# A GRU recurrence turned from hidden units on partitions to sequences on partitions

## The chip, the core and the metric

The kernel is one program on one core of a Trainium2 chip. Its engines run side by side, each through its own list of instructions, and meet at semaphores: PE (TensorE, matmuls), DVE (VectorE), ACT (ScalarE), POOL (GpSimd) and SP (SyncE, which here only issues DMAs). The metric is the time of one execution on the device in microseconds.

## What is computed

Input x has 16 sequences of 256 steps and 512 features. Layer 0 adds a feed-forward block to x: a conditioning vector for each sequence (attention over block sums, projected) is added, the rows are normalised, quantised in blocks of 32, and go through gate, up and down matrices (512 to 2048 and back), quantised again in between. Layer 1 runs a GRU over the 256 steps and adds a linear layer with 16 low-rank experts, of which a router picks two. The part that the change touches is the GRU:

```python
def cell(h, x):
    gi = x @ W_ih + b_ih
    gh = h @ W_hh + b_hh
    i_r, i_z, i_n = jnp.split(gi, 3, axis=-1)
    h_r, h_z, h_n = jnp.split(gh, 3, axis=-1)
    r = jax.nn.sigmoid(i_r + h_r)
    z = jax.nn.sigmoid(i_z + h_z)
    n = jnp.tanh(i_n + r * h_n)
    h_new = (1.0 - z) * n + z * h
    return (h_new, h_new)
```

Here h is 16 by 512 and W_hh is 512 by 1536. Each step needs the state of the step before, so 256 steps follow one another.

## The kernel before

The work is cut into 32 tiles of 128 rows, a row being one sequence at one step, so a tile holds 8 steps. Every engine walks through slots (c, s), where c is the tile in recurrence and s from 0 to 7 is its step. Beside step s of tile c a slot holds pieces of the other stages for neighbouring tiles: Q (normalising and quantising tile c+4), F (feed-forward of tile c+3), E (the end of the feed-forward and x1 of tile c+2), I (the input product x1 @ W_ih of tile c+1), R (the recurrence of tile c) and L (the expert layer of tile c-1). The order on each engine is the order in which `slot` and `others` write it. There is no scheduler, and no instruction passes another of its engine.

The recurrence before keeps hidden units on partitions. W_hh is the stationary operand in 128 by 128 pieces, and 32 columns stream past each: 16 columns of the high half of the state in half precision and 16 of its low half. Weights are split in two halves as well. A step takes 3 gates times 4 output pieces times 4 inner pieces times 2 halves, 96 matmuls (`state_products`, L1248, called at L1282 to L1284). The gates r and n lie in `ps_rn`, z lies in `ps_z`. DVE (`recur`, L709) adds the two halves and the input terms, ACT takes three tanh, and DVE forms the new state with 64 numbers on each of 128 partitions, rounds it (`hT`, L753) and takes the low half (L704), for which PE waits (L1280).

The input product `x_wih` (L1139) has W_ih stationary and 128 columns of x1 moving, 144 matmuls for a tile. ACT moves its result out with bias and scale (L512), so that `gi` lies with units on partitions, as the recurrence wants it. The scale of x1 is one number for the tile: a row maximum on DVE (L852), a turn of it by PE (`max_row`, L1108), a maximum over the row (L856), and a matmul that spreads the result (`spread_scale`, L1115). Four fp32 transposes turn x1 (L1125), and ACT and DVE split it in halves out of PSUM (L499, L901).

On DVE, `others(c, s, 0)` stands ahead of the step's first instruction, and places 1, 2 and 3 stand after the first additions, after `n_pre` and after the new state. Below, place 0 to 3 has this meaning.

## Time and profile before

| | |
|---|---|
| median of 3 runs | 1842.02 us (1841.2 to 1842.82) |
| profiled execution, own time | 1841.74 us |
| its span in the trace | 1839.9 us |
| PE busy | 1609.0 us, 87% of the span |
| PE weight loads busy | 1252.7 us, 68% |
| DVE busy | 1511.1 us, 82% |
| ACT busy | 661.5 us, 36% |
| POOL busy | 511.7 us, 28% |

Busy time is the union of an engine's instructions, and an engine that is busy need not be at its best rate. The first 326 us load, quantise and fill the pipeline of stages, then the 256 steps run to 1821 us. Rows of the trace below give times in microseconds from the start of the span, and L numbers are lines of the kernel before.

### The profile page before, as it was taken

Reading aid. Unit: us, or ns where it says so; the run is one execution under the profiler, and the core shown is the slowest. Engines: PE = TensorE matmul, PEld = TensorE weight load, DVE = VectorE, ACT = ScalarE, POOL = GpSimd, SP = SyncE. Lnnn points to the kernel's source line nnn. Section 1 sums busy time; section 2 is a strip of 40 time slices with the busy share of each in tenths; the row PEclk is TensorE's granted clock in tenths of the full one; section 3 lists DMA queues with packets and bytes.
Section 4 is the critical chain, followed back from the end, with each engine's and each line's share of the span. In section 5 each row is a group of like instructions: output and inputs, shape, how many; then the busy total and the mean of one; then the engine's idle time right before and its main releaser. Section 6 shows DMA issues by size and latency. Waiting matters only on the chain.

```text
span 1839.9 us, 76467 instructions
## 1 busy us (share of the span) xinstructions
PE 1609.0 (87%) x32972; PEld 1252.7 (68%) x32972; DVE 1511.1 (82%) x5651; ACT 661.5 (36%) x1712; POOL 511.7 (28%) x571
## 2 busy tenths in 40 slices
PE   5422246899999999999999999999999999999986
PEld 2211114788777777877777777787777877778874
DVE  8999988888888888888888888888888888887654
ACT  1111123444443434344343444434434344334331
POOL 4445423222222222222222222222222222221001
PEclk8755568999999999999999999999999999999997
DMA  6413121000100010000000100000000000000000
GB/s 250 162 63 132 54 92 32 29 9 32 31 32 32 32 32 32 32 32 32 32 26 31 32 32 31 32 32 32 32 32 32 32 31 32 26 26 24 22 15 19
DMA packets 35411, 80.12 MB, mean 44 GB/s; under 512 B 4865, under 2 KB 5249, under 8 KB 34689
## 3 DMA queue, kind: packets, MB, share of 16 engines
q1 hardware_dynamic: 28080, 63.09, 9.8%
q10 hardware_dynamic: 6992, 12.13, 1.9%
q8 instruction: 260, 4.26, 1.0%
q14 instruction: 79, 0.64, 0.1%
HBM read 58.43 MB, written 16.78 MB: 41 GB/s over the span
## 4 chain that ended last, share of the span: by engine, by line
PE 72%; DVE 23%; issue 2%; ACT 1%; DMA 1%; POOL 0%; DVEq 0%; ACTq 0%; SPq 0%; POOLq 0%
PE ps_rn L1254 22%; PE ps_gi L1148 11%; PE ps_z L1254 9%; PE ps_gate_up L1087 6%; PE ps_down L1105 6%; PE ps_base L1157 4%; PE ps_gate_up L1081 4%; PE ps_base L1201 3%; PE ps_route L1157 3%; DVE gi L567 2%; DVE gi L564 1%; DVE wam L541 1%; DVE gi L569 1%; DVE wm L564 1%; DVE fe L766 1%
## 5 line engine op out<-in xcount | busy, mean ns | idle before, releaser
L1254 PE MATMUL ps_rn<-hT,whh 128*128 128x32 f16 x16320 | 449.0, 176 | 37.1 <-DVE hT L704 37.0
L1254 PEld LDWEIGHTS ps_rn<-hT,whh 128*128 128x128 f16 x16320 | 434.9, 96 | 63.6 <-DVE hT L704 56.2
L976 POOL TENSOR_TENSOR qf<-f8c,fe 128x512 bf16<-128x512 bf16 x128 | 135.6, 1059 | 902.5 <-DVE f8c L783 885.8
L1148 PE MATMUL ps_gi<-x1T,wih 128*128 128x128 f16 x4608 | 288.6, 219 | 1.2 <-ACT gi L512 1.2
L1148 PEld LDWEIGHTS ps_gi<-x1T,wih 128*128 128x128 f16 x4608 | 270.3, 98 | 25.7 <-issue 1.7
L521 ACT ACTIVATE r_tanh<-r_pre,scale_half 128x64 f32<-128x64 f32 x256 | 89.0, 348 | 452.1 <-DVE r_pre L724 452.1
L1254 PE MATMUL ps_z<-hT,whh 128*128 128x32 f16 x8160 | 243.3, 176 | 0.0
L1254 PEld LDWEIGHTS ps_z<-hT,whh 128*128 128x128 f16 x8160 | 222.7, 96 | 0.0
L512 ACT ACTIVATE gi<-ps_gi,b_i,scale_x 128x128 f32<-128x128 f32 x384 | 144.4, 456 | 200.7 <-PE ps_gi L1148 200.7
L718 DVE TENSOR_TENSOR r_half<-ps_rn,gi 128x64 f32<-128x64 f32 x256 | 56.6, 221 | 143.8 <-PE ps_rn L1254 143.7
L1081 PE MATMUL ps_gate_up<-wq,qxT 128*128 128x512 bf16 x512 | 136.0, 389 | 13.3 <-DVE inter L798 13.3
L523 ACT ACTIVATE z_tanh<-z_pre,scale_half 128x64 f32<-128x64 f32 x256 | 89.0, 348 | 161.3 <-DVE z_pre L734 161.3
L1087 PE MATMUL ps_gate_up<-wq,qxT 128*128 128x512 bf16 x512 | 138.2, 394 | 2.1 <-ACT sg_gs L472 2.1
L1105 PE MATMUL ps_down<-wq,qfT 128*128 128x512 bf16 x512 | 133.3, 383 | 0.0
L1157 PE MATMUL ps_base<-wl,hT 128*128 128x512 f16 x384 | 97.1, 391 | 0.0
L525 ACT ACTIVATE n<-n_pre,scale_half 128x64 f32<-128x64 f32 x256 | 89.0, 348 | 12.3 <-DVE n_pre L741 1.0
L798 DVE TENSOR_TENSOR inter<-ps_gate_up,sg_gs 128x512 f32<-128x512 f32 x128 | 87.3, 682 | 7.2 <-PE ps_gate_up L1087 7.0
L759 DVE TENSOR_REDUCE fam<-inter 128x16 f32<-128x512 f32 x128 | 87.8, 686 | 4.4
L472 ACT ACTIVATE sg_gs<-ps_gate_up 128x512 f32<-128x512 f32 x128 | 74.1, 579 | 42.8 <-PE ps_gate_up L1081 42.8
L777 DVE SCALAR_TENSOR_TENSOR f<-inter,finv 128x512 fp8e4<-128x512 f32 x128 | 87.6, 684 | 0.0
L1087 PEld LDWEIGHTS ps_gate_up<-wq,qxT 128*128 128x128 bf16 x512 | 43.1, 99 | 59.9 <-issue 27.5
L1105 PEld LDWEIGHTS ps_down<-wq,qfT 128*128 128x128 bf16 x512 | 48.4, 99 | 49.5 <-issue 4.1
(200 smaller groups left out, 2680.2 us busy)
## 6 DMA issues: line engine op xcount, KB each, us to landing
wih<-in_x_steps ACTq DMA_DIRECT2D x32, 256.0 KB, 5.3
xin<-in_x_steps SPq DMA_DIRECT2D x32, 256.0 KB, 3.5
...
```

The costliest lines, as they stand in the source:

```text
L512: last = nc.scalar.activation(gi_gate(i, g)[:, k, :], ps_gi[:, k * P:(k + 1) * P], ACT.Identity, bias=b_i[:, g * KD + k:g * KD + k + 1], s ...
L521: nc.scalar.activation(r_tanh[:, :], r_pre[:, :], ACT.Tanh, scale=HALF_S_INV).then_inc(r_ok, 1)
L523: nc.scalar.activation(z_tanh[:, :], z_pre[:, :], ACT.Tanh, scale=HALF_S_INV).then_inc(z_ok, 1)
L525: nc.scalar.activation(n[:, :], n_pre[:, :], ACT.Tanh, scale=HALF_S_INV).then_inc(n_ok, 1)
L759: v.tensor_reduce(am[:, :], blocked(src[:, :]), AX_X, ALU.max, apply_absolute_value=True).then_inc(small, 1)
L976: g.tensor_tensor(blocked(qf[:, :]), blocked(f8c[:, :]), spread(fe16[:, :]), ALU.mult).then_inc(qf_done, 1)
L1081: last = mm(ps_gate[:, :], qxT[:, k, :], w_ffn(0, n, k), start=k == 0, stop=k == KD - 1)
L1087: last = mm(ps_up[:, :], qxT[:, k, :], w_ffn(8, n, k), start=k == 0, stop=k == KD - 1)
L1105: last = mm(ps_down[:, :], qfT[:, i, :], w_down(i), start=i == 0, stop=i == NF * KD - 1)
L1148: last = mm(ps_gi[:, j * P:(j + 1) * P], wih_parts[:, k, at:at + P], x1T[:, x, k, :], start=k + w + x == 0, stop=k == KD - 1 and w == 1)
L1157: last = mm(out, hT[l % 2][:, 2 * k + x, :], wl_parts[:, k, begin:begin + n], start=k + w + x == 0, stop=stop and w == 1)
L1254: last = mm(ps[:, (at + j) * 2 * B:(at + j + 1) * 2 * B], whh[:, k, u, gate * D + j * P:gate * D + (j + 1) * P], hx(t)[:, 2 * k:2 * k + 2, ...
```

## The change

Sequences go on partitions in the recurrence. The 512 hidden units are four groups of 128, and group g of all 16 sequences lies on partitions 32g to 32g+15. The state is now stationary (16 columns) and W_hh streams: 384 columns (three gates of one group) for each matmul. The four groups write to four column tiles of the PE array, partitions 0, 32, 64 and 96 of one PSUM bank. A step is 48 matmuls: high state by high weights and high state by low weights (32 of them), a wait for the low state, and low state by high weights (16). Two banks `ps_gru` alternate. DVE works on 128 columns for each gate: one addition of 256 columns for r and z, one of 128 for n, and at the end a 32 by 32 block transpose of the new state, from which both halves are taken.

The input product now has x1 stationary and W_ih moving with 512 columns, 36 matmuls a tile. DVE moves its result out (place 0 of steps 2, 4, 6), rows on partitions. Since a step needs its 16 rows on the partitions of the four groups, SP sends four DMAs of 24 KB for each step, from `gi` to a ring of four steps, two slots ahead. The scale of x1 is one number for each row, so that PE's two small matmuls and their way back go. x1 is split in halves before it is turned, by ACT and DVE, and eight half-precision transposes turn it. Biases are spread by matmuls once, ahead of the recurrence, and weights are loaded in another order of rows. The load of x1 for the expert layer and its result share one tile, and its load moves from slot 0 to slot 2 on SP.

```diff
+GROUPS, GROUP = 4, 32
+RING = 4
...
-        ps_rn, ps_z, ps_up, ps_down = bank("ps_rn"), bank("ps_z"), bank("ps_gate_up"), bank("ps_down")
+        ps_gru = bank("ps_gru0"), bank("ps_gru1")
+        ps_up, ps_down = bank("ps_gate_up"), bank("ps_down")
...
+        gi_ring = sb("gi_ring", [P, RING, 4 * P])
+        h, hT_both = sb("h", [P, P]), sb("hT_both", [P, KD, GROUP])
...
+            def load_gi(t):
+                c, s = t // STEPS, t % STEPS
+                sp.wait_ge(gi_ev, count(c, 3, 3))
+                wait(sp, n_pre_ok, t - RING + 1)
+                if t < RING:
+                    sp.wait_ge(ring_clear, 1)
+                for g in range(GROUPS):
+                    sp.dma_start(gi_ring[g * GROUP:g * GROUP + B, t % RING, 0:3 * P],
+                                 gi_tokens(c)[s * B:(s + 1) * B, g, :, :].rearrange("p q f -> p (q f)"))\
+                        .then_inc(gi_in[t % RING], 16)
...
+                if 0 <= c * STEPS + s + 2 < T:
+                    load_gi(c * STEPS + s + 2)
...
+                if (c, s) == (-2, 7):
+                    act.wait_ge(wih_lo, KD)
+                    for gate in range(3):
+                        act.wait_ge(bias_mm, gate + 1)
+                        nc.scalar.activation(gi_bias[:, gate * D:(gate + 1) * D], (ps_gi, *ps_gru)[gate][:, :], ACT.Copy,
+                                             scale=S_WH).then_inc(bias_ok, 1)
...
+                if E and s == 6:
+                    act.wait_ge(x_small, count(e, 6, 5))
+                    wait(act, x_mm, count(e, 1))
+                    nc.scalar.activation(x1_parts[:, 0, :], x1[:, :], ACT.Copy, scale=S_X[:, :]).then_inc(x_hi, 1)
                 if E and s == 7:
-                    act.wait_ge(x_scale_mm, count(e, 1, 1))
-                    wait(act, x_ev, count(e, 1))
-                    wait(act, gi_ev, count(e, 3))
-                    nc.scalar.activation(scale_x[:, :], ps_x_scale, ACT.Copy).then_inc(x_scale_ok, 1)
                     act.wait_ge(x_mm, count(e, 1, 1))
                     wait(act, gi_mm, count(e, 3))
-                    act.wait_ge(x_scale_ok, count(e, 1, 1))
-                    nc.scalar.activation(x1T[:, 0, :, :], ps_turn[:, :].rearrange("p (k n) -> p k n", k=KD),
-                                         ACT.Copy, scale=S_X).then_inc(x_hi, 1)
+                    nc.scalar.activation(x1T[:, :, :, :], turn_x.rearrange("p (u k n) -> p u k n", u=2, k=KD),
+                                         ACT.Copy).then_inc(x_ev, 1)
...
-                    for k in range(KD):
-                        last = nc.scalar.activation(gi_gate(i, g)[:, k, :], ps_gi[:, k * P:(k + 1) * P], ACT.Identity,
-                                                    bias=b_i[:, g * KD + k:g * KD + k + 1], scale=X_TO_WH)
-                    last.then_inc(gi_ev, 1)
...
+                    t = c * STEPS + s
+                    act.wait_ge(rz_pre_ok, t + 1)
+                    nc.scalar.activation(r_tanh[:, :], pre[:, 0:P], ACT.Tanh, scale=HALF_S_INV).then_inc(r_ok, 1)
+                    nc.scalar.activation(z_tanh[:, :], pre[:, P:2 * P], ACT.Tanh, scale=HALF_S_INV).then_inc(z_ok, 1)
+                    act.wait_ge(n_pre_ok, t + 1)
...
+            def state_parts(t):
                 dve.wait_ge(h_ok, t + 2)
-                v.tensor_tensor(h_part(t, 1), by_chunk(h[:, :]), h_part(t, 0), ALU.subtract).then_inc(hx_ok, 1)
-            def gi_step(c, gate, s):
-                return gi_gate(c, gate)[:, :, s * B:(s + 1) * B]
+                v.transpose(hT_both[:, :, :].rearrange("p k b -> p (k b)"), h[:, :]).then_inc(h_turned, 1)
+                dve.wait_ge(h_turned, t + 2)
+                v.tensor_copy(h_part(t, 0), hT_both[:, :, 0:B]).then_inc(hx_hi, 1)
+                dve.wait_ge(hx_hi, t + 2)
+                v.tensor_tensor(h_part(t, 1), hT_both[:, :, 0:B], h_part(t, 0), ALU.subtract).then_inc(hx_ok, 1)
...
+                t = c * STEPS + s
+                dve.wait_ge(gh_mm, t + 1)
+                dve.wait_ge(gi_in[t % RING], (t // RING + 1) * GROUPS * 16)
+                if t < RING:
+                    dve.wait_ge(bias_ok, 3 + RING)
+                v.tensor_tensor(pre[:, 0:2 * P], ps_gru[t % 2][:, 0:2 * P], gi_step(t)[:, P:3 * P],
+                                ALU.add).then_inc(rz_pre_ok, 1)
+                v.tensor_tensor(pre[:, 2 * P:3 * P], ps_gru[t % 2][:, 2 * P:3 * P], gi_step(t)[:, 3 * P:4 * P],
                                 ALU.add).then_inc(hn_ok, 1)
                 beside(1)
+                dve.wait_ge(hn_ok, t + 1)
+                dve.wait_ge(r_ok, t + 1)
+                v.scalar_tensor_tensor(rn[:, :], r_tanh[:, :], 1.0, pre[:, 2 * P:3 * P], ALU.add,
+                                       ALU.mult).then_inc(rn_ok, 1)
+                dve.wait_ge(rn_ok, t + 1)
+                v.scalar_tensor_tensor(n_pre[:, :], gi_step(t)[:, 0:P], 2.0, rn[:, :], ALU.mult,
                                        ALU.add).then_inc(n_pre_ok, 1)
                 beside(2)
                 if s == 0:
                     wait(dve, base_mm, c - 1)
+                dve.wait_ge(z_ok, t + 1)
                 v.tensor_scalar(less_z[:, :], z_tanh[:, :], 1.0, HALF_S_H, ALU.subtract, ALU.mult)
                 v.scalar_tensor_tensor(zh[:, :], z_tanh[:, :], 1.0, h[:, :], ALU.add, ALU.mult).then_inc(zh_ok, 1)
+                dve.wait_ge(zh_ok, t + 1)
+                dve.wait_ge(n_ok, t + 1)
                 v.tensor_tensor(zn[:, :], less_z[:, :], n[:, :], ALU.mult).then_inc(zn_ok, 1)
+                dve.wait_ge(zn_ok, t + 1)
                 v.scalar_tensor_tensor(h[:, :], zh[:, :], 0.5, zn[:, :], ALU.mult, ALU.subtract).then_inc(h_ok, 1)
+                state_parts(t)
...
+                if E and here == (6, 3):
+                    dve.wait_ge(x_hi, count(e, 1, 1))
+                    v.scalar_tensor_tensor(x1_parts[:, 1, :], x1[:, :], S_X[:, :], x1_parts[:, 0, :], ALU.mult,
+                                           ALU.subtract).then_inc(x_lo, 1)
+                if I and place == 0 and s in (2, 4, 6):
+                    g = s // 2 - 1
+                    dve.wait_ge(gi_mm, count(i, 3, g + 1))
+                    if c == -1:
+                        dve.wait_ge(bias_ok, 3)
+                    v.scalar_tensor_tensor(gi_tokens(i)[:, :, gi_place(g), :], ps_gi[:, :].rearrange("p (g f) -> p g f", g=GROUPS),
+                                           x_to_wh[i % 2][:, :], gi_bias[:, g * D:(g + 1) * D].rearrange("p (g f) -> p g f", g=GROUPS),
+                                           ALU.mult, ALU.add).then_inc(gi_ev, 1)
...
-                mm(ps_x_row, row_max[:, :], idf[:, :], start=True, stop=True).then_inc(x_row_mm, 1)
...
-                mm(ps_x_scale, ones_row[:, :], x_row[:, :], start=True, stop=True).then_inc(x_scale_mm, 1)
...
+                for u in range(2):
+                    for k in range(KD):
+                        at = (u * KD + k) * P
+                        last = turn_(turn_x[:, at:at + P], x1_parts[:, u, k * P:(k + 1) * P], idh[:, :])
...
+                for k in ks:
+                    for w, x in PART_PRODUCTS:
+                        at = w * GATES + n * D
+                        last = mm(ps_gi[:, :], x1T[:, x, k, :], wih_parts[:, k, at:at + D], start=k + w + x == 0,
+                                  stop=k == KD - 1 and w == 1)
...
+            def state_products(t):
+                def by_group(w, u):
                     for k in range(KD):
+                        gates = whh[:, k, w, :].rearrange("p (q g f) -> p q g f", q=3, g=GROUPS)
+                        for g in range(GROUPS):
+                            last = mm(ps_gru[t % 2][g * GROUP:g * GROUP + B, 0:3 * P], hx(t - 1)[:, 2 * k + u, :],
+                                      gates[:, :, g, :], start=k + w + u == 0, stop=u == 1 and k == KD - 1)
+                    return last
+                by_group(0, 0)
+                by_group(1, 0)
+                pe.wait_ge(hx_ok, t + 1)
+                by_group(0, 1).then_inc(gh_mm, 1)
...
+                    t = c * STEPS + s
+                    wait(pe, hn_ok, t - 1)
+                    pe.wait_ge(hx_hi, t + 1)
+                    state_products(t)
...
```

PE, ahead of a middle tile's step 5 and up to step 6. First before: `ps_rn` and `ps_z` are the 96 state products, `ps_gi` the input product.

```order
L1254 MATMUL ps_rn<-hT,whh 128x32 x64
L1254 MATMUL ps_z<-hT,whh 128x32 x32
L1113 MATMUL ps_route<-idf,row_max 1x128
L1087 MATMUL ps_gate_up<-wq,qxT 128x512 x4
L1105 MATMUL ps_down<-wq,qfT 128x512 x4
L1148 MATMUL ps_gi<-x1T,wih 128x128 x24
L1254 MATMUL ps_rn<-hT,whh 128x32 x64
```

The same place of PE after the change, where `ps_gru` holds the 48 state products.

```order
L1258 MATMUL ps_gru<-whh,hT 16x384 x48
L1111 MATMUL ps_gate_up<-wq,qxT 128x512 x4
L1129 MATMUL ps_down<-wq,qfT 128x512 x4
L1158 MATMUL ps_gi<-wih,x1T 128x512 x6
L1258 MATMUL ps_gru<-whh,hT 16x384 x48
```

The turn of the row maximum is gone, 96 narrow matmuls became 48 wide ones, and 24 of the input product became 6.

DVE before, step 6 of a middle tile: from the place 0 pieces to the low half of the state.

```order
L798 TENSOR_TENSOR inter<-ps_gate_up,sg_gs 128x512
L759 TENSOR_REDUCE fam<-inter 128x16
L838 TENSOR_TENSOR wxa<-xa,coeff 128x256
L856 TENSOR_REDUCE x_max<-ps_route 1x1
L718 TENSOR_TENSOR r_half<-ps_rn,gi 128x64
L720 TENSOR_TENSOR hn_half<-ps_rn,b_h 128x64
L724 TENSOR_TENSOR r_pre<-ps_rn,r_half 128x64
L727 TENSOR_TENSOR hn<-ps_rn,hn_half 128x64
```

DVE after, the same place; `pre_activations` is the sum of state product and ring.

```order
L817 TENSOR_TENSOR inter<-ps_gate_up,sg_gs 128x512
L778 TENSOR_REDUCE fam<-inter 128x16
L857 TENSOR_TENSOR wxa<-xa,coeff 128x256
L882 TENSOR_SCALAR x_scale<-x_inverse 128x1
L883 TENSOR_SCALAR x_to_wh<-x_power,scale_l 128x1
L894 SCALAR_TENSOR_TENSOR gi<-ps_gi,x_to_wh,wih 128x4x128
L750 TENSOR_TENSOR pre_activations<-ps_gru,gi_ring 128x256
L752 TENSOR_TENSOR pre_activations<-ps_gru,gi_ring 128x128
```

A third of the input product's way out now stands ahead of the step's first addition, and two additions took the place of four.

The end of the same step on DVE after the change:

```order
L772 TENSOR_TENSOR zn<-less_z,n 128x128
L774 SCALAR_TENSOR_TENSOR h<-zh,zn 128x128
L736 STREAM_TRANSPOSE hT_both<-h 128x128
L738 CAST hT<-hT_both 128x4x16
L740 TENSOR_TENSOR hT<-hT_both,hT 128x4x16
L887 SCALAR_TENSOR_TENSOR x_parts<-x,x_scale,x_parts 128x512
```

Between the new state and the half that PE waits for, a transpose and a rounding now stand, and the low half of x1 follows at place 3.

## Rows read from the trace of the kernel before

**Rows 1.** Page part 5: line, engine, shapes, count; busy us, mean ns; idle before, releaser.

```profile
L1254 PE MATMUL ps_rn<-hT,whh 128*128 128x32 f16 x16320 | 449.0, 176 | 37.1 <-DVE hT L704 37.0
L1254 PEld LDWEIGHTS ps_rn<-hT,whh 128*128 128x128 f16 x16320 | 434.9, 96 | 63.6 <-DVE hT L704 56.2
```

**Rows 2.** Windows: stretch, its length, then PE, PEld, DVE, ACT, POOL busy; clock; DMA.

```profile
300.00:350.00 50.00, 45.24 (x827) 34.91 (x825) 43.32 (x136) 22.44 (x53) 15.76 (x16) 0.97 0.07 24
...
1750.00:1800.00 50.00, 39.21 (x1097) 33.96 (x1094) 29.27 (x154) 16.21 (x48) 2.69 (x6) 0.93 0.05 13
...
1000.00:1200.00 200.00, 196.93 (x4311) 158.14 (x4308) 164.29 (x703) 81.24 (x221) 54.52 (x67) 1.00 0.09 29
```

**Rows 3.** Source L704, low half of the state: durations, first and last start.

```profile
L704 DVE TENSOR_TENSOR hT<-h,hT x256: 224/225/227, 326.2 to 1820.7; 128x64 f16<-128x64 f32 x128
```

**Rows 4.** Timeline of PE, one tile: start, length, group, count, [idle before].

```profile
1005.32 1.77 PE L1254 MATMUL ps_rn<-hT,whh 128*128 128x32 f16 x64 [0.59 <-DVE hT L704]
...
1007.73 1.02 PE L1087 MATMUL ps_gate_up<-wq,qxT 128*128 128x512 bf16 x4
...
1014.71 1.50 PE L1148 MATMUL ps_gi<-x1T,wih 128*128 128x128 f16 x24
1016.05 0.81 PE L1157 MATMUL ps_base<-wl,hT 128*128 128x512 f16 x3
...
1019.18 0.38 PE L1113 MATMUL ps_route<-idf,row_max 128*1 128x128 f32 x2
1019.49 1.04 PE L1087 MATMUL ps_gate_up<-wq,qxT 128*128 128x512 bf16 x4
1020.36 1.03 PE L1105 MATMUL ps_down<-wq,qfT 128*128 128x512 bf16 x4
...
1052.86 1.77 PE L1254 MATMUL ps_rn<-hT,whh 128*128 128x32 f16 x64 [0.59 <-DVE hT L704]
```

**Rows 5.** Waits from 1001.4 to 1048.95: who waited for whom, total, times, longest.

```profile
DVE r_half L718 <- PE ps_rn L1254: 3.8, 5, 1.3
...
DVE x1T L901 <- ACT x1T L499: 1.3, 1, 1.3
```

**Rows 6.** Timeline of DVE, one step of the tile.

```profile
1007.12 0.22 DVE L718 TENSOR_TENSOR r_half<-ps_rn,gi 128x64 f32<-128x64 f32 x1 [0.73 <-PE ps_rn L1254]
1007.26 0.21 DVE L720 TENSOR_TENSOR hn_half<-ps_rn,b_h 128x64 f32<-128x64 f32 x1
...
1010.12 0.22 DVE L755 SCALAR_TENSOR_TENSOR h<-zh,zn 128x64 f32<-128x64 f32 x1
1010.38 0.22 DVE L704 TENSOR_TENSOR hT<-h,hT 128x64 f16<-128x64 f32 x1
```

**Rows 7.** Lines by form, 600 to 1600 us: shapes, count; busy, mean ns; idle.

```profile
L777 DVE SCALAR_TENSOR_TENSOR f<-inter,finv 128x512 fp8e4<-128x512 f32 x85 | 58.2, 684 | 0.0
...
L472 ACT ACTIVATE sg_gs<-ps_gate_up 128x512 f32<-128x512 f32 x84 | 48.5, 577 | 0.0
...
L897 DVE SCALAR_TENSOR_TENSOR y<-ps_base,scale_l,x_bias 128x512 f32<-128x512 f32 x21 | 15.8, 751 | 0.0
```

**Rows 8.** Timeline of all engines near the end, one step with nothing beside it.

```profile
1785.09 1.79 PE L1254 MATMUL ps_rn<-hT,whh 128*128 128x32 f16 x64 [0.73 <-DVE hT L704]
...
1786.91 0.23 DVE L718 TENSOR_TENSOR r_half<-ps_rn,gi 128x64 f32<-128x64 f32 x1 [1.69 <-PE ps_rn L1254]
...
1788.63 0.35 ACT L525 ACTIVATE n<-n_pre,scale_half 128x64 f32<-128x64 f32 x1
...
1790.02 1.79 PE L1254 MATMUL ps_rn<-hT,whh 128*128 128x32 f16 x64 [2.33 <-DVE hT L704]
```

**Rows 9.** Timelines of DVE and of GpSimd where both run.

```profile
1001.95 0.88 DVE L766 TENSOR_SCALAR fe<-fam 128x16 f32<-128x16 f32 x1
...
1001.53 1.27 POOL L988 TENSOR_TENSOR xg<-xg,beta_b 128x512 f32<-128x512 f32 x1
```

**Rows 10.** DMA issues: KB each, us from issue to landing.

```profile
h<-in_h SPq DMA_DIRECT2D x1, 32.0 KB, 1.6
```

274 lines of the change are left out of this document (105 added, 169 removed).

## The prediction

> **What bounds the kernel now.** I read the costliest groups first. The state products wait 37 us in all for the low half of the state [rows 1], of 256 steps. Then the windows: from 1000 to 1200 us PE is busy 196.9 of 200 and DVE 164.3 [rows 2]. The 256 steps lie between 326.2 and 1820.7 us [rows 3]. In the timeline of PE one tile of eight steps runs from 1005.32 to 1052.86, 47.54 us, with one idle gap of 0.59 [rows 4]. The reader is to see PE going from one group to the next. So PE sets the end in a middle tile, but DVE is close behind it: in this tile it waits 3.8 us for `ps_rn` and 1.3 for ACT's turned x1 [rows 5], and fills the other 42.4 us with work and short gaps. Near the end no other stage is left, and a step takes 4.93 us, from PE's start at 1785.09 to 1790.02 [rows 8]: that is the loop itself, products, additions, tanh, new state. 29 tiles at 47.54 and 23 steps at 4.93 make 1492 of the 1494.5 us between first and last state, which is how I use the two figures.
>
> So there are three limits for a tile: PE's work (47.0), DVE's work and the waits that it cannot fill, and the loop (8 times 4.93, 39.4). The change lowers the first and raises the other two.
>
> **PE's part.** The 96 products take 2.41 us (1005.32 to 1007.73) [rows 4]. The new ones stream 12 rounds of 384 columns, if the four column tiles run side by side. A 512-column matmul takes 0.217 (four in 0.87, from 1019.49 to 1020.36) [rows 4], so 384 take 0.163 and a round no less: 1.95 us a step. That saves 0.46, 3.7 a tile. The row-maximum matmul takes 0.31 (1019.18 to 1019.49) [rows 4]; with the other one like it, 0.6 a tile. The input product: 24 matmuls of 128 columns take 1.34 (1014.71 to 1016.05) [rows 4], 144 take 8.0, and 36 of 512 columns 7.8: 0.2. Four fp32 turns against eight in half precision I count even. PE's tile goes from 47.0 to 42.5 us.
>
> No row shows a column tile. The bounds for one step are 1.95 us (all four together) and 48 times 0.163, 7.8 us (none together). I take 1.95, because weight loads last 96 ns each [rows 1] where a load and its matmul follow every 0.025 us (64 in 1.6), so several are under way at once, and four independent tiles need one pair started only every 0.041.
>
> **DVE's part.** In the step at 1007.12 an instruction of 64 columns starts 0.14 after one that it does not need and 0.26 after one that it needs (1010.12 to 1010.38) [rows 6]. A 512-column one lasts 0.684 against 0.22 [rows 6, 7], 1.04 ns a column; 64 more columns are 0.07, 192 more 0.20. Before, a step has 14 instructions, 9 of the first kind and 5 of the second: 2.56 us. After there are 11: the sum for r and z 0.34; hn, `n_pre`, `less_z` 0.21 each; rn, zh, zn, h and the transpose 0.33 each, since each is needed at once; high half 0.26; low half 0.14. That is 3.02, so 0.46 more a step, 3.7 a tile. The input product's way out leaves ACT, which had room, and costs DVE three times 0.67 (0.751 long as `y` [rows 7], less the overlap of 0.08 that the rows show between a length of 0.22 and a distance of 0.14), 2.0 a tile. The low half of x1 replaces an equal one. The small scale steps lose some 0.2. Occupied: 42.4 + 3.7 + 2.0 - 0.2 = 47.9 us, already above the old tile.
>
> Waits that DVE cannot fill: from the sum's start to r's tanh in hand are 0.42 + 0.40 + about 0.10 in hand-overs, 0.92 (tanh of 64 columns lasts 0.35 [rows 8], 512 columns 0.577 [rows 7]; 0.40 is my estimate for 128). DVE has 0.55 of its own there; 0.37 stays in steps 1, 3 and 7, which have nothing at place 1: 1.1. In step 3 place 0 is short (1.2) and PE's results come 2.14 after its start: 0.7. In step 6 the low half of x1 waits for ACT, whose turn comes after tanh, silu and two copies: 0.4. Together 2.2. Two waits of before go: `ps_rn`, since DVE now arrives later than PE nearly everywhere, and x1T. The tile comes to 50.1 us, 2.55 longer, over 29 tiles 74 us.
>
> The three pieces of `gi` stand at place 0 of steps 2, 4 and 6, ahead of the sum that starts the loop. Behind them in DVE's queue waits the whole step, for which ACT and PE wait in turn. Step 6 has inter, its maxima, wxa and `gi` there, over 3 us against 2.14 for PE. So the saving on PE buys nothing in these steps: late next is DVE.
>
> **The unknown prices on DVE.** The transpose of 128 by 128 fp32: at least the 0.26 of a 64-column instruction, at most the 0.72 of a 512-column one; I take 0.33 because it reads and writes 128 columns. This leaves -18 to +100 us over 256 steps. The conversion of the high half may be held up: `fe` takes 0.88 instead of some 0.17 when it starts at 1001.95 inside a GpSimd instruction from 1001.53 to 1002.80 [rows 9]. GpSimd is busy 54.5 of 200 us [rows 2]; a hold of 0.35 on average in 27% of 256 steps is 25 us, against 0. I keep it in the range.
>
> **The loop, where nothing else runs.** Before 4.93. After: products 1.95 and 0.19 until DVE has them, as `r_half` starts 1.82 after PE's start with 1.63 of products ahead of it [rows 8]; r's tanh in hand 0.92; rn 0.33; `n_pre` to n in hand 0.79; zn, h, transpose 1.0; high half and PE's start 0.28. Sum 5.46, 0.53 more. The loop now needs all three gates before the first addition, where r and n alone used to do. 23 steps make 12 us.
>
> **What hides.** 1024 new DMAs of 24 KB: the load of `h`, 32 KB, landed 1.6 us after its issue [rows 10], and they go out two slots (12 us) ahead. At a tile's edge SP stands at the store of y until DVE's last instruction of step 7, and the next ring load behind it still has two slots. Cost 0; without the cover up to 2 us a tile, 64. ACT has less to do (its copies of `gi` go, x1T is one copy of 1024 columns); cost 0. Ahead of the first step come 16 matmuls to spread biases, seven ACT copies, a memset and 27 more load DMAs, in a stretch where PE is busy 45.2 of 50 and DVE 43.3 [rows 2]. I take 5 us, from 0 to 12.
>
> **Sum.** 74 + 12 + 5 = 91 on the profiled execution's own 1841.7 us (span 1839.9): 1933. The median of the runs, 1842.0, differs by 0.3 and changes nothing.
>
> **Two rules that speak against it.** The loads of 128 columns overlap matmuls on the same rows of the array [rows 1, 4]. The Trainium skill, TensorE: Matmul & The Clock Gate, Part 3, says that a weight load overlaps matmuls in flight only when its row group differs; the four column tiles share all rows, so by that rule the first rival below would come. By it the trace would not show what it shows, and its table nevertheless has three column tiles running 2.38 times faster, which no run here shows yet.
>
> PE's result is there 0.176 us after the start of a 32-column matmul, of which 0.025 is its turn [rows 1]; so emptying the array costs up to 0.15, and twice a step. The Trainium skill, TensorEngine Tiling (Array Packing), Key Properties, says that a change of tiling mode drains the engine. One of the two falls in time in which PE waits anyway. The other is off the loop and takes 1.2 a tile of the 7.6 that PE has over. It would add some 5 to 10 us to 1933.
>
> **Rival 1: the tiles do not run side by side.** Then a step is 7.8 + 0.19 + 3.32, with 0.3 of DVE's delays 11.6 us, times 256, and 351 around them: 3320. In favour: nothing in the trace shows them together. Against: the overlapping loads. If they overlap by two, products take 3.9, a step about 7.7, and the time is 2320; with 2.5 to 3 us it is 1990 to 2100, since DVE's place 0 covers the first half microsecond. The skill's rule on row groups, above, leads to 3320.
>
> **Rival 2, the other side: wide instructions cost DVE little more than narrow ones.** The mechanism is the fixed part, 0.14 of distance, if width counted only beyond it. If the chain's 128-column instructions cost what those of 64 do, a step loses 0.8, the tile falls under 44, PE's 42.5 and its drains become the bound, and 29 tiles save some 100 us: about 1750. It decides from 0.32 us a step on. Against it stands 0.684 for 512 columns. A smaller error of mine, or pieces that fill waits better, would end between 1790 and 1838.
>
> **Rival 3: the clock.** It is 1.00 with PE at 98%, 0.97 at 45.2 of 50 and 0.93 at 39.2 of 50 [rows 2], and 1.2 GHz is its lower level. PE will work 42.5 of 50 us. At 0.95 its products lengthen by 0.1 a step, 25 us: 1960.
>
> **How the numbers follow.** DVE-bound as worked out, 1885 to 1990, rival 3 in it: 0.62. The same with less loss, 1846 to 1885: 0.06. Partly overlapping tiles, 1990 to 2500: 0.13. None overlapping: 0.07. Faster (rival 2 and its smaller forms): 0.10. Within 0.2%, about what a measurement of this kernel can tell from no change: 0.02. So faster 0.10, same 0.02, slower 0.88. The range 1855 to 2110 leaves out the serial case, the faster one and the far end of the partial one.
>
> **What would show it.** The period of a middle tile near 50 (not 47.5, not 44); PE idle 5 to 7 us of it, before the state products, with DVE's conversion as releaser; 48 products in about 2.1 us; the sums on DVE waiting for PE only in steps 0 and 3; the transpose near 0.28 long; the last steps 5.4 to 5.5 apart. A period under 47 with DVE waiting would refute the DVE ledger; products over 3 us the overlap; a sum released by a DMA the cover.

## The result, and the profile after

The changed kernel takes 1974.91 us (median of 4 runs, 1971.5 to 1976.78) against 1841.61 us (1838.99 to 1842.82) for the kernel before: a ratio of 1.0724, 95% interval 1.071 to 1.0738. It is 133 us slower. Predicted were 1933 us, range 1855 to 2110, with a chance of 0.88 for slower. In the profiled execution the span is 1969.5 us.

First the page after, part 5 as in [rows 1], and one row of part 6:

```profile
L1258 PE MATMUL ps_gru<-whh,hT 128*16 128x384 f16 x12240 | 568.4, 337 | 230.7 <-DVE hT L738 229.5
L1258 PEld LDWEIGHTS ps_gru<-whh,hT 128*16 128x16 f16 x12240 | 311.0, 91 | 499.3 <-issue 357.5
...
L750 DVE TENSOR_TENSOR pre_activations<-ps_gru,gi_ring 128x256 f32<-128x256 f32 x256 | 107.2, 419 | 92.0 <-PE ps_gru L1258 89.7
...
L758 DVE SCALAR_TENSOR_TENSOR rn<-r_tanh,pre_activations 128x128 f32<-128x128 f32 x256 | 77.2, 301 | 39.7 <-ACT r_tanh L559 36.9
L761 DVE SCALAR_TENSOR_TENSOR n_pre<-gi_ring,rn 128x128 f32<-128x128 f32 x256 | 99.4, 388 | 8.8
...
L736 DVE STREAM_TRANSPOSE hT_both<-h 128x128 f32<-128x128 f32 x257 | 80.0, 311 | 8.8
...
gi_ring<-gi SPq DMA_DIRECT2D x1024, 24.0 KB, 1.9
```

PE's wait for the state has grown from 37 to 230 us: the bound has moved off PE. `n_pre` is 388 ns on average where its neighbours of the same width are 295 to 301; that is the first hint of what the prediction did not place. The chain that ended last (page part 4) gives the same picture; before, PE had 72% of it and DVE 23%:

```profile
DVE 61%; PE 21%; issue 9%; ACT 7%; DMA 1%; DVEq 0%; POOL 0%; ACTq 0%; SPq 0%; POOLq 0%
```

The low half of the state (L740 now; columns as in [rows 3]) shows where the time lies:

```profile
L740 DVE TENSOR_TENSOR hT<-hT_both,hT x256: 224/224/228, 326.5 to 1950.3; 128x64 f16<-128x64 f32 x128
```

The first state comes 0.3 us later than before, the end 19.2 us after the last as before, and the 256 steps take 129.3 us more. Eight starts of that line are one tile. The first tile takes 56.1 us (before 47.7), the next 27 tiles 51.17 on average (before 47.57; 50.6 in some, 51.9 to 52.2 in about every third), the last three together 140.9 (before 126.6), and the last seven steps 45.2 (before 35.9). So 8.5 + 97.3 + 14.3 + 9.3 us.

The windows (columns as in [rows 2]), first two short ones inside a tile that takes 52 us:

```profile
1006.00:1009.40 3.40, 1.21 (x6) 0.36 (x4) 3.12 (x10) 1.27 (x4) 1.46 (x2) 1.00 0.01 3
1009.40:1012.80 3.40, 2.83 (x36) 1.36 (x40) 1.65 (x5) 0.25 (x2) 1.05 (x1) 0.50 0.33 87
...
1000.00:1200.00 200.00, 174.63 (x2052) 87.57 (x2051) 176.15 (x570) 61.09 (x154) 50.27 (x61) 0.98 0.15 43
```

In 200 us PE is busy 174.6 instead of 196.9, DVE 176.2 instead of 164.3. The two short windows are step 2 and the start of step 3 of that tile. Here are DVE, then POOL (GpSimd), then PE in that place (start, length, instruction, idle before it):

```profile
1004.75 0.42 DVE L750 TENSOR_TENSOR pre_activations<-ps_gru,gi_ring 128x256 f32<-128x256 f32 x1
1005.08 0.28 DVE L752 TENSOR_TENSOR pre_activations<-ps_gru,gi_ring 128x128 f32<-128x128 f32 x1
1005.28 0.93 DVE L785 TENSOR_SCALAR fe<-fam 128x16 f32<-128x16 f32 x1
1006.24 0.17 DVE L787 TENSOR_SCALAR finv<-fe 128x16 uint32<-128x16 uint32 x1
1006.33 1.25 DVE L790 TENSOR_SCALAR fe<-fe 128x16 uint32<-128x16 uint32 x1
1007.49 0.28 DVE L758 SCALAR_TENSOR_TENSOR rn<-r_tanh,pre_activations 128x128 f32<-128x128 f32 x1
```
```profile
1004.91 1.27 POOL L1011 TENSOR_TENSOR xg<-xn,gamma_b 128x512 f32<-128x512 f32 x1 [4.91 <-DVE xn L907]
1006.26 1.29 POOL L1013 TENSOR_TENSOR xg<-xg,beta_b 128x512 f32<-128x512 f32 x1
```
```profile
1009.97 3.50 PE L1258 MATMUL ps_gru<-whh,hT 128*16 128x384 f16 x48 [2.77 <-DVE hT L738]
1013.40 0.82 PE L1111 MATMUL ps_gate_up<-wq,qxT 128*128 128x512 bf16 x3
```

Two operations on 16 columns take 0.93 and 1.25 us, where the same lines take 0.17 in other steps. Each starts inside a GpSimd pass over 512 columns and ends 0.03 us after that pass (1006.18 and 1007.55). The whole chain of the step stands behind them. PE runs out of work, idles for 2.77 us, and the granted clock is 0.50 (1.2 GHz) from 1009.4 to 1012.8, so the next 48 products take 3.50 us instead of 2.13. In step 7 the same happens to an operation of the chain itself:

```profile
1039.45 0.40 DVE L758 SCALAR_TENSOR_TENSOR rn<-r_tanh,pre_activations 128x128 f32<-128x128 f32 x1 [0.34 <-ACT r_tanh L559]
1039.89 1.24 DVE L761 SCALAR_TENSOR_TENSOR n_pre<-gi_ring,rn 128x128 f32<-128x128 f32 x1
```
```profile
1038.66 1.05 POOL L1001 TENSOR_TENSOR qf<-f8c,fe 128x512 bf16<-128x512 bf16 x1 [5.71 <-DVE f8c L802]
1039.66 1.31 POOL L994 TENSOR_TENSOR xs<-xin,proj 128x512 f32<-128x512 f32 x1
```

Added up, these holds are 0.76 + 1.08 + 0.12 + 0.95 = 2.9 us a tile (0.12 is `rn` above, which starts inside the first of the two passes). They come in every tile from the second to the 27th, 2.8 to 2.9 us in all but one. The clock does not fall in every tile: it falls behind step 2 in 9 of the 27 middle tiles.

What DVE waits for, 600 to 1700 us, some 21.5 tiles:

```profile
DVE pre_activations L750 <- PE ps_gru L1258: 31.9, 22, 2.5
...
DVE rn L758 <- ACT r_tanh L559: 21.8, 64, 0.3
DVE x_parts L887 <- ACT x_parts L543: 7.0, 21, 0.3
```

That is 0.34 for r's tanh in three steps of a tile, 0.33 for the high half of x1 in one, and one wait for the products a tile, in step 3 (the prediction had expected it in step 0 too). No wait for a DMA is among them. And a step of the tail, with nothing beside the loop:

```profile
1899.60 2.13 PE L1258 MATMUL ps_gru<-whh,hT 128*16 128x384 f16 x48 [1.59 <-DVE hT L738]
...
1901.78 0.42 DVE L750 TENSOR_TENSOR pre_activations<-ps_gru,gi_ring 128x256 f32<-128x256 f32 x1 [1.40 <-PE ps_gru L1258]
...
1902.74 0.29 DVE L758 SCALAR_TENSOR_TENSOR rn<-r_tanh,pre_activations 128x128 f32<-128x128 f32 x1 [0.34 <-ACT r_tanh L559]
...
1905.24 0.99 PE L1258 MATMUL ps_gru<-whh,hT 128*16 128x384 f16 x20 [1.77 <-DVE hT L738]
```

From product to product 5.64 us; before it was 4.93 [rows 8].

### The profile page after: what moved, and what is told of

The parts are those of the page before. It is cut to its first block, busy times and chain, and to the rows that moved or that the text cites. A ratio compares the mean times of both kernels' runs of the same rounds, so it can differ in the third digit from the quotient of the medians.

```text
span 1969.5 us, 45556 instructions
## 1 busy us (share of the span) xinstructions
PE 1543.6 (78%) x17268; PEld 773.2 (39%) x17268; DVE 1689.1 (86%) x4947; ACT 559.1 (28%) x1335; POOL 521.4 (26%) x573
## 4 chain that ended last, share of the span: by engine, by line
DVE 61%; PE 21%; issue 9%; ACT 7%; DMA 1%; DVEq 0%; POOL 0%; ACTq 0%; SPq 0%; POOLq 0%
PE ps_gru L1258 14%; DVE n_pre L761 5%; DVE pre_activations L750 4%; DVE rn L758 3%; DVE hT_both L736 3%; DVE inter L817 3%; DVE zn L772 3%; DVE h L774 3%; DVE gi L894 3%; ACT n L562 2%; ACT r_tanh L559 2%; PE ps_route L1167 2%; DVE hT L738 2%; DVE fe L790 2%; DVE f L796 2%
## 5 line engine op out<-in xcount | busy, mean ns | idle before, releaser
L1258 PE MATMUL ps_gru<-whh,hT 128*16 128x384 f16 x12240 | 568.4, 337 | 230.7 <-DVE hT L738 229.5
L1258 PEld LDWEIGHTS ps_gru<-whh,hT 128*16 128x16 f16 x12240 | 311.0, 91 | 499.3 <-issue 357.5
L559 ACT ACTIVATE r_tanh<-pre_activations,scale_half 128x128 f32<-128x128 f32 x256 | 102.8, 401 | 920.4 <-DVE pre_activations L750 920.4
L1158 PE MATMUL ps_gi<-wih,x1T 128*128 128x512 f16 x1152 | 280.3, 379 | 1.3 <-DVE gi L894 1.3
L750 DVE TENSOR_TENSOR pre_activations<-ps_gru,gi_ring 128x256 f32<-128x256 f32 x256 | 107.2, 419 | 92.0 <-PE ps_gru L1258 89.7
L562 ACT ACTIVATE n<-n_pre,scale_half 128x128 f32<-128x128 f32 x256 | 102.7, 401 | 207.2 <-DVE n_pre L761 207.2
L1158 PEld LDWEIGHTS ps_gi<-wih,x1T 128*128 128x128 f16 x1152 | 109.5, 98 | 118.2 <-issue 3.5
L761 DVE SCALAR_TENSOR_TENSOR n_pre<-gi_ring,rn 128x128 f32<-128x128 f32 x256 | 99.4, 388 | 8.8
L560 ACT ACTIVATE z_tanh<-pre_activations,scale_half 128x128 f32<-128x128 f32 x256 | 98.9, 386 | 0.0
L736 DVE STREAM_TRANSPOSE hT_both<-h 128x128 f32<-128x128 f32 x257 | 80.0, 311 | 8.8
```

Of the source, the lines that this page charges most:

```text
L559: nc.scalar.activation(r_tanh[:, :], pre[:, 0:P], ACT.Tanh, scale=HALF_S_INV).then_inc(r_ok, 1)
L562: nc.scalar.activation(n[:, :], n_pre[:, :], ACT.Tanh, scale=HALF_S_INV).then_inc(n_ok, 1)
L736: v.transpose(hT_both[:, :, :].rearrange("p k b -> p (k b)"), h[:, :]).then_inc(h_turned, 1)
L750: v.tensor_tensor(pre[:, 0:2 * P], ps_gru[t % 2][:, 0:2 * P], gi_step(t)[:, P:3 * P], ALU.add).then_inc(rz_pre_ok, 1)
L761: v.scalar_tensor_tensor(n_pre[:, :], gi_step(t)[:, 0:P], 2.0, rn[:, :], ALU.mult, ALU.add).then_inc(n_pre_ok, 1)
L1158: last = mm(ps_gi[:, :], x1T[:, x, k, :], wih_parts[:, k, at:at + D], start=k + w + x == 0, stop=k == KD - 1 and w == 1)
```

## The experiments

All kernels but e16 and e18 start from the changed kernel. e1, e2, e3, e4, e12 and e16 leave something out or compute something else; the others compute everything. "Tile" is the mean of the second to the 28th tile of the recurrence in the profiled execution, the ratio is to the kernel before, timed on the same chip. The changed kernel has 1974.9 us, 1.0724 and 51.17.

| run | us | ratio, 95% interval | tile |
|---|---|---|---|
| e1_one_column_tile | 3337.1 (one run) | | 93.64 |
| e2_no_transpose | 1910.2 | 1.0368 (1.0351 to 1.0386) | 49.41 |
| e3_gate_inputs_by_scalar | 1924.2 | 1.0439 (1.0422 to 1.0456) | 49.67 |
| e4_no_shared_hold | 1900.2 | 1.0310 (1.0292 to 1.0327) | 48.93 |
| e5_keep_clock | 1953.8 | 1.0625 (1.0607 to 1.0642) | 50.60 |
| e6_reordered | 1894.7 | 1.0298 (1.0281 to 1.0315) | 48.63 |
| e8_all_together | 1904.9 | 1.0356 (1.0338 to 1.0373) | 49.05 |
| e10_early_split | 1974.2 | 1.0727 (1.0709 to 1.0745) | 51.32 |
| e12_fewer_products | 1942.8 | 1.0545 (1.0523 to 1.0567) | 50.92 |
| e13_bias_on_tensor | 1868.7 | 1.0139 (1.0121 to 1.0158) | 47.85 |
| e16_before_no_hold | 1814.4 | 0.9843 (0.9825 to 0.9861) | 46.85 |
| e18_before_reordered | 1819.9 | 0.9880 (0.9863 to 0.9896) | 46.86 |

**e1: one column tile.**

```diff
-mm(ps_gru[t % 2][g * GROUP:g * GROUP + B, 0:3 * P], ..., start=k + w + u == 0, ...)
+mm(ps_gru[t % 2][0:B, 0:3 * P], ..., start=k + w + u + g == 0, ...)
```

> The 48 state products of a step all go to the same column tile (partitions 0 to 31 of the bank) instead of four; everything else stays, and the state is then computed from sums that mix the four gate groups. Theory (the four column tiles run side by side; a step's 48 products take 2.06 us at 337 ns each, so four are in work at a time): one after another they take 3.5 to 7.8 us (48 x 160 ns for 384 columns at 2.4 GHz = 7.7 us), the step goes from 6.3 to 11 or 12 us, and the whole run to 3000 to 3400 us. Rival (the 2.06 us comes from short moving operands, not from tiles side by side): no change, about 1975 us.

```profile
1010.29 7.96 PE L1258 MATMUL ps_gru<-whh,hT 128*16 128x384 f16 x48 [0.90 <-DVE hT L738]
```

The same 48 matmuls take 7.96 us instead of 2.13, a factor of 3.7, and the kernel takes 3337 us. So the four tiles do run side by side, which the prediction had taken without a row for it. Its first rival is refuted by the changed kernel, and its price (3320 us) confirmed by this one. The rule of the Trainium skill that the prediction weighed against it (TensorE: Matmul & The Clock Gate, Part 3, a weight load overlaps matmuls only when its row group differs) does not hold for these column tiles: all four use the same rows, and 48 weight loads of 91 ns, 4.4 us if one followed another, go by in the 2.13 us.

**e2: no transpose.**

```diff
-v.transpose(hT_both[:, :, :].rearrange("p k b -> p (k b)"), h[:, :]).then_inc(h_turned, 1)
+if t < 0:
+    v.transpose(...).then_inc(h_turned, 1)
```

> Left out: the turn of the new state on VectorE (0.311 us in the trace) in all 256 steps; the parts of the state are cut from the old turned copy. Theory (VectorE's sum of a tile sets the period, and the turn is part of it): minus 0.33 us x 256 = minus 84 us, some 1890 us. Rival A (the loop over TensorE sets it in all steps and the turn lies in it too): the same minus 84, but the tile's wait of VectorE for the products grows. Rival B (VectorE waits for others anyway, the turn is cover): within 20 us of 1975. Should the clock fall more often in shorter steps, up to 20 us of the gain go back.

Minus 65 us, between the theory and its rival B: 1.8 us a tile of the 2.5 that eight transposes last. DVE's wait for the products rose from 31.9 to 40.4 us in 600 to 1700 us, so a part turned into waiting for PE, and the wait for the high half of x1 rose from 7.0 to 14.9.

**e3: gate inputs moved out by ScalarE.**

```diff
-v.scalar_tensor_tensor(gi_tokens(i)..., ps_gi..., x_to_wh[i % 2][:, :], gi_bias..., ALU.mult, ALU.add)
+nc.scalar.activation(gi_tokens(i)..., ps_gi..., ACT.Copy, scale=x_to_wh[i % 2][:, :])
```

> The three evictions of gate inputs a tile (0.74 us each on VectorE, 512 columns, with the bias added) go to ScalarE as a scaled copy behind steps 1, 3 and 5; the input biases of the three gates are left out. Theory (VectorE's sum sets the tile): minus 3 x 0.74 = 2.2 us a tile, less what opens as a new wait in steps 2, 4 and 6 (0.3 a tile), x 30 = minus 57 us, some 1918 us. Rival (ScalarE's extra 0.6 us in a step lands before a tanh of the recurrence, and the eviction was cover for the wait for the products): minus 20 us or less.

Minus 51 us, 1.5 a tile of 2.2. Again DVE then waits more for PE (48.2 us in the same stretch). In e2 and in e3 the gap of PE before step 3 is shorter than in the changed kernel (2.1 us instead of 2.77 in most tiles), and yet the clock falls there in 13 and in 15 of the 27 middle tiles instead of 9. ACT had room, as forecast.

**e4: GpSimd's two passes on 16 columns.**

```diff
-g.tensor_tensor(xg[:, :], xn[:, :], gamma_b[:, :], ALU.mult)
+g.tensor_tensor(xg[:, 0:16], xn[:, 0:16], gamma_b[:, 0:16], ALU.mult)
```

The pass with beta in the same way.

> GpSimd's two passes over the normalised input (times gamma, plus beta) work on 16 columns of 512, so the front stage gets wrong inputs; VectorE's and TensorE's work is as in the changed kernel. Theory (in step 2 these two passes hold VectorE: the small exponent operation takes 0.93 us instead of 0.17 and n_pre 1.24 instead of 0.29, and TensorE, left without work for 2.8 us by it, falls to 1.2 GHz in every second or third tile, which makes step 3's products 3.7 us instead of 2.1): minus 1.7 us x 31 and minus 17 us for the clock, some 1905 us. Rival (the holds only take the place of waits that come anyway, TensorE's clock has another cause): within 15 us of 1975.

Minus 75 us with no work taken from DVE or PE: 2.2 a tile (60 in 27 tiles), 5 in the first tile and 5 ahead of the first step. The passes themselves are shorter here, which e6 leaves out of the question. The hold of `n_pre` in step 7 is still there (1.24 us), since it comes from another pass. The falls of the clock before step 3 go too: after 350 us the clock is at 0.5 for 34 us in all instead of 71.5.

**e5: the clock alone.**

```diff
+WARM = {3: 10}
...
+if t >= 8 and s in WARM:
+    for _ in range(WARM[s]):
+        mm(ps_gru[t % 2][:, :], idb[:, :], wq[:, 0:1, 0:512], start=True, stop=True)
 pe.wait_ge(hx_hi, t + 1)
```

> Ten more matmuls of 512 columns in step 3 of each tile, before TensorE's wait for the new state, into the bank that the step's own products overwrite; nothing is left out. Theory (part of the missing time is TensorE's clock, which in every second or third tile falls to 1.2 GHz for 3.41 us after 2.8 us without work in front of step 3): the granted clock stays at 1.0 there, every tile takes 50.6 us instead of 50.6 or 52.1, minus 10 to 20 us in all, some 1958 us. Rival (the clock has another cause than the gap in front of step 3): the falls stay, and the ten matmuls, where they end behind the state, cost up to 2 us a tile: 1975 to 2030 us.

```profile
1000.84 2.11 PE L1311 MATMUL ps_gru<-wq,idb 128*128 128x512 bf16 x9
1003.46 2.13 PE L1259 MATMUL ps_gru<-whh,hT 128*16 128x384 f16 x48 [0.51 <-DVE hT L739]
```

The extra matmuls fill most of the gap, the products stay at 2.13, and nearly all tiles take 50.5. Minus 21 us: 0.57 a tile of the 3.6 lost is the clock. The clock falls in none of the 27 middle tiles any more, so the fall comes of the gap before it: filling the gap, with nothing else changed, removes it.

**e6: both holds, with nothing left out.**

```diff
-if Q and here == (2, 0):
+if Q and here == (1, 3):
...
     v.tensor_scalar(xn[:, :], xs[:, :], mv[:, 0:1], rstd[:, 0:1], ALU.subtract, ALU.mult)
...
+if R and c:
+    pool.wait_ge(hx_ok, c * STEPS + 1)
 g.tensor_tensor(xs[:, :], xin[:, :], proj[:, :], ALU.add)
```

> Nothing is left out: VectorE normalises the front stage's input one place earlier (behind step 1's state instead of in step 2), so that GpSimd's two passes over it run under VectorE's operations that read PSUM, and GpSimd's first pass of a tile waits for step 7's state to be cut, so that it runs in step 0. Theory (GpSimd holds VectorE's exponent operation and n_pre in step 2, and n_pre in step 7, and TensorE's clock falls behind step 2's hold): minus 1.7 us in step 2, minus 0.9 in step 7, and minus 17 us for the clock, some 1885 us; if the early normalisation delays step 2 no more than it frees. Rival (whatever VectorE does beside GpSimd is held alike): no more than 15 us off 1975.

Minus 80 us. The GpSimd passes are as long as before (1.29 and 1.27) and run under other work of DVE, from `inter` to the sums out of PSUM. Only the end of the second still meets `fe`, which takes 0.33 instead of 0.93:

```profile
966.38 1.29 POOL L1013 TENSOR_TENSOR xg<-xn,gamma_b 128x512 f32<-128x512 f32 x1 [2.93 <-DVE xn L907]
967.75 1.27 POOL L1015 TENSOR_TENSOR xg<-xg,beta_b 128x512 f32<-128x512 f32 x1
```
```profile
968.72 0.33 DVE L785 TENSOR_SCALAR fe<-fam 128x16 f32<-128x16 f32 x1
969.09 0.18 DVE L787 TENSOR_SCALAR finv<-fe 128x16 uint32<-128x16 uint32 x1
969.17 0.17 DVE L790 TENSOR_SCALAR fe<-fe 128x16 uint32<-128x16 uint32 x1
```

**e10: the expert weights split a tile earlier,** on ACT and on DVE.

```diff
-if c == 0 and s < KD:
+if c == -1 and s < KD:
...
```

> Nothing is left out: the expert weights are split into high and low parts one tile earlier (before the recurrence, in place of steps 0 to 3 of its first tile). Theory (the first tile of the recurrence took 56.1 us, 5 us over the others, because VectorE makes the low parts there): that tile takes 51 us, the ramp grows by 0 to 5 us, the time falls by 0 to 5 us: 1970 to 1975 us. Rival (it is long because its evictions and loads come late): it stays at 56 us and the ramp grows, 1975 to 1980 us.

The first tile falls from 56.1 to 51.5 us as the theory says, and the ramp takes it back (first low half at 330.8 instead of 326.5). Work on a bound engine was moved, not hidden. The split is not the whole of the first tile's loss: in e6, which leaves it in place, that tile takes 51.6, 3.0 over the later ones. One difference is the clock, which is at 0.50 for 13.7 us in the first tile of the changed kernel and for 3.4 in e6's.

**e12: a third of the state products left out.**

```diff
 by_group(0, 0)
-by_group(1, 0)
```

> Left out: the products of the state's high part with the weights' low part, 16 of a step's 48 state products (0.65 us of TensorE a step, also on the loop). Theory (VectorE's own sum sets the steps, only one or two of eight are set by the loop): 1 to 2 us a tile, and more time at the low clock in the longer gaps, 1930 to 1975 us. Rival (TensorE's products are on the path of every step): minus 0.65 x 256 = minus 166 us, some 1810 us.

Minus 32 us: 0.25 a tile in the middle (7 in all), 4 in the first tile and the other 21 in the last three tiles and the seven steps after them, where little but the loop is left. Here the clock works against it: each gap before step 3 is 3.6 us long now, the clock falls in 26 of the 27 middle tiles, and it is low for 141 us instead of 71.5. So PE's own time was worth little in the middle of the changed kernel; what it would be worth there without the falls was not run.

**e8 and e13: how far the new form goes.** Both have e6 and e10, and in both the r, z and state biases are added by one more matmul a step, ahead of the wait, so that `hn` is not summed on DVE, and ACT moves the r and z inputs out:

```diff
+mm(ps_gru[t % 2][:, 0:3 * P], picks_h[:, :], b_rows[:, :], start=True, stop=False)
 pe.wait_ge(hx_hi, t + 1)
...
-v.tensor_tensor(pre[:, 2 * P:3 * P], ps_gru[t % 2][:, 2 * P:3 * P], gi_step(t)[:, 3 * P:4 * P], ALU.add)
```

In e8 the clipping of the feed-forward also moves, in odd steps:

```diff
-if s % 2 == 1 and place == 0:
-    if there:
+if s % 2 == 1 and there:
+    if place == 0:
         to_f8(f_small, at * 4, f8, inter, finv, f8_done)
-    if there:
+    if place == 1:
         clip(f8c, f8, f8_done, at, qf_done, f8c_done)
```

> Nothing is left out. Together: the order of e6_reordered, the early split of e10_early_split, the clipping of the feed-forward stage moved beside ScalarE's r tanh (VectorE waits 0.34 us for it in steps 1, 3 and 7), the state bias and the r and z biases added by one more matmul of 384 columns a step, before TensorE's wait for the state, so that VectorE's addition of the state bias (0.29 us a step) goes and r x n reads PSUM, and the gate inputs of r and z moved out by ScalarE (0.74 us each). Theory (VectorE's sum sets the tile): minus 2.6 (holds), 2.3 (state bias), 1.4 (gate inputs), 1.0 (waits for r), plus 0.5 for waits that open: 51.2 to 45.4 us a tile, against some 45.0 for eight steps of the bare loop of 5.63 us; in all minus 31 x 5.8 = minus 180, some 1795 us. Rival (the loop takes over earlier, and TensorE's clock falls more often in the gaps): 47.5 us a tile, 1860 us.

The theory failed: 1905 us, 10 more than e6 alone. The trace has one reason in steps 1, 3, 5 and 7:

```profile
821.77 1.05 POOL L1025 TENSOR_TENSOR qf<-f8c,fe 128x512 bf16<-128x512 bf16 x1 [7.79 <-DVE f8c L824]
821.83 0.29 DVE L780 SCALAR_TENSOR_TENSOR rn<-r_tanh,ps_gru 128x128 f32<-128x128 f32 x1
822.15 0.82 DVE L783 SCALAR_TENSOR_TENSOR n_pre<-gi_ring,rn 128x128 f32<-128x128 f32 x1
```

The later clipping lets GpSimd start later, and its pass lands on `n_pre` (two SBUF inputs), not on `rn`, which now reads PSUM. `fe` in step 2 is held again too, 0.78 us instead of 0.17 (at 827.38).

> Nothing is left out. As e8_all_together, but the clipping stays where the changed kernel has it. e8 was slow since the later clipping let GpSimd's pass behind it hold n_pre in steps 1, 3, 5 and 7 (0.8 us instead of 0.29) and since VectorE, with less to do, waited for the products (76 us in 1100 us). Theory: the holds go (minus 2.0 us a tile), VectorE then waits 0.6 us for r tanh in the three steps that have nothing beside it; 46.0 to 46.8 us a tile against 48.5 in e6_reordered, some 1820 to 1840 us, with 45.0 (eight bare loops of 5.63) as the floor. Rival (the loop through TensorE binds wherever VectorE's sum falls, and the extra matmul lengthens it by 0.1 to 0.2 a step): 47.5 to 48.5 us a tile, 1860 to 1890 us.

With the clipping back, 1868.7 us, 47.85 a tile: above the theory's 1820 to 1840, inside the rival's 1860 to 1890. So the place of the clipping accounts for some 36 of the 110 us by which e8 missed its forecast. The holds of `n_pre` are gone, and PE is late:

```profile
906.43 2.11 PE L1182 MATMUL ps_gi<-wih,x1T 128*128 128x512 f16 x9
908.47 0.33 PE L1334 MATMUL ps_gru<-b_rows,picks_h 64*128 64x384 f16 x1
908.73 2.13 PE L1282 MATMUL ps_gru<-whh,hT 128*16 128x384 f16 x48
```

Here the state's high half was ready at 908.05, and PE came to it at 908.73, from the input product of the slot before. In 1000 to 1200 us PE is busy 194 of 200, which makes 46.4 of a tile's 47.85, and eight bare loops of the tail take 45. So by these two figures little more is to be had without taking work off PE.

**e16 and e18: the kernel before.** e16 is the kernel before with e4's edit, e18 the kernel before with e6's edit and nothing left out.

> The kernel before, with GpSimd's two passes over the normalised input on 16 columns of 512 (the front stage gets wrong inputs). Theory (these passes cost 1.7 us a tile only since VectorE sets the tile; before, TensorE did, and a held VectorE was covered): within 8 us of 1841. Rival (the holds cost the kernel before as much): minus 50 to 75 us, as in e4_no_shared_hold.

> The kernel before with the two moves of e6_reordered and nothing else: VectorE normalises the front stage's input behind step 1's state, and GpSimd's first pass of a tile waits until the state of the last tile's end is cut. Nothing is left out. Theory (e16_before_no_hold showed that GpSimd's two passes cost the kernel before 0.7 us a tile through the exponent operation in step 2, 0.88 us instead of 0.17, and 3 us in the first tile; moved under operations that read PSUM they cost nothing): 46.8 us a tile, 1812 to 1820 us, faster than the kernel before and than every other run here. Rival (the earlier normalisation delays step 2's state products, which TensorE has no slack for): 1840 us or more.

e16 lies between its theory (within 8 us) and its rival (50 to 75): the passes cost the kernel before 29 us, 0.7 a tile (19), 3 in the first tile and 4 ahead of the first step. `fe` in step 2 is 0.88 there [rows 9], and PE, which was taken to cover it, stood for it with the 0.59 gap of [rows 4]; in e16 that gap is gone. e18 gets most of this without leaving work out, 1819.9 us, as its theory said (1812 to 1820); it is the fastest kernel of this study that computes everything. The best of the new form, e13, is 49 us above it: with e6's edit in both, sequences on partitions remain the slower form as far as they were carried here. PE in e18 has no gap that the window shows:

```profile
1000.00:1200.00 200.00, 200.00 (x4375) 161.20 (x4373) 165.88 (x725) 81.39 (x222) 53.78 (x71) 1.00 0.09 31
```

## Why the prediction was right, and where not

*DVE becomes the bound: right.* PE idles before the state products with DVE's conversion as releaser, as forecast, and e2, e3 and e4, which relieve DVE or what holds it, each win 51 to 75 us, while e12, which relieves PE, wins 32, of which only 7 lie in the 27 middle tiles.

*PE's part: the products right, the tile a little low.* 48 products last 2.13 us, and the next group starts 2.05 after them (971.74 to 973.79 in e6), against 1.95 in the sum; the draining that was allowed for is at most this 0.1 a step. e1 shows that the price of the serial case was right too. PE's tile was to fall from 47.0 to 42.5. In e6, whose clock stays up, PE is busy 182.7 us of 200, which makes 44.4 of a tile's 48.6, against 46.8 before. The saving is 2.4 and not 4.5: the state products save some 3.0 instead of 3.7, and the input product takes 8.5 (before 8.2) instead of 7.8. With DVE the bound this did not touch the time, but it is what e13 runs into.

*DVE's ledger: the sum nearly right, by luck in part.* The tile was to be 50.1 us and is 50.6 at full clock. The wide chain was to cost 3.7 more a tile. Taken as eight times the median distance from each of its starts to the next start on DVE, over ten middle tiles, it costs 3.1 more (24.4 in e6 against 21.3 before). The eviction of the gate inputs was 2.0, and is 1.97. The base of 42.4 already held 1.2 us of holds of the kernel before, 0.7 of `fe` and 0.5 of `wxa`, which took 0.875 us there and takes 0.415 (median) in the changed kernel:

```profile
L838 DVE TENSOR_TENSOR wxa<-xa,coeff x21: 871/875/882, 642.8 to 1594.1; 128x256 f32<-128x256 f32 x21
```

Such holds move with the timing and are no work of DVE. In their place the changed kernel has 2.9. e6, where the holds are nearly gone, has a tile of 48.6, 1.5 under the forecast; the holds that it moves are worth 2.0 of the 50.6. So 1.5 us too much in work and waits stood against 2.0 of holds that were in no term, and the half microsecond that is left is not a measure of how good the ledger was.

*Waits: 2.2 forecast,* measured 1.0 (r), 0.33 (x1) and 0.9 to 2.5 (step 3): 2.2 where the clock holds.

*The step of the prediction that failed is the one on holds by GpSimd.* It put them on the conversion of the state and on chance (0 to 25 us, by the share of GpSimd's time) and took 0 in the sum. The conversion is never held (194 to 243 ns over 256 steps). 33 of them start inside a GpSimd operation of 16 columns and some 0.5 us (`c`, at 414.3 for one, with 0.42 us of it left) and last 0.24 at most, so that one does not hold them. None starts inside a pass of 512 columns, in any of these traces, so whether such a pass would hold a conversion stays open. What is held is fixed by the order of work and comes in each middle tile: two small operations in step 2 and `n_pre` in step 7. The Trainium skill, SBUF — State Buffer, "Who interferes with whom", says that a VectorE instruction with two SBUF inputs contends with a GpSimd instruction that reads SBUF, and that the one issued first keeps the ports to its end. By that rule `n_pre` (two SBUF inputs) had to be on the list and the sums out of PSUM not; the traces of the changed kernel and of e8 agree, 1.24 and 0.82 us against 0.29, ending 0.15 after GpSimd's pass, while `rn` in e8, with one input in PSUM, lies inside the same pass and takes 0.29. It also says that a `tensor_scalar` in a mode that takes both ports contends with GpSimd; `fe` agrees, 0.93 and 1.25 against 0.17, though the trace does not name the mode. Moving the passes (e6) took 80 us off: 2.0 a tile of holds and 0.57 of the clock in the middle tiles.

*The clock: a cost of the size of rival 3, by another way.* Rival 3 had 0.95 on average, 25 us. The fall is local: 0.50 for some 3.4 us in step 3 of 9 of the 27 middle tiles, behind a gap that the hold makes. e5 prices it at 21 us, 15 of them in the middle tiles. It was in the range and not in the sum.

*The first tile: missed.* The split of the expert weights, four operations of 832 columns on DVE, lay under PE before. With DVE the bound, taking it out of that tile is worth 4.6 us there (56.1 against 51.5 in e10). "What was hidden, and by what" has to be asked again for work that the change does not touch.

*The loop: 5.46 forecast, 5.63 measured.* Products to DVE 2.18 for 2.14, r in hand 0.96 for 0.92, n in hand 0.83 for 0.79, conversion and PE's start 0.34 for 0.28: each hand-over 0.04 to 0.06 longer. Over 23 steps this adds 4 us to the 12. Six of these steps take 6.7 to 7.3 us, with the clock at 0.50 for 3.4 us in each, together 8.5 more. Against that, the kernel before also took 2.2 more than 23 times 4.93, and the 29th tile grew by 0.7 instead of 2.55. The end came out 9 over the forecast.

*The ramp: 5 forecast, 0.3 measured. DMAs: 0, and 0 measured,* 1.9 us to landing and nobody waits.

Added: 1933, plus 13 for the middle tiles (27 times the 0.5 between 50.1 and e5's 50.60), 15 for the clock in them (27 times 0.57), 6 for the first tile beyond its 2.55, 9 for the tail, less 5 for the ramp, makes 1971. The profiled execution took 1971.5; the median lies 3.4 above it.

*Rival 2 (width costs little): wrong.* Operations of 128 columns stay 0.28 to 0.29 long, and those of 256 0.42, against 0.22 for 64.

*Left open:* why the clock falls in some tiles and not in others with the same 2.77 us gap, and more often behind the 2.1 us of e2 and e3, is not shown; and a PE order balanced over the eight slots, which e13 points to, was not run.
